# A pre-activation convolution on one core: transformed planes and sums with the columns outside and the row quadruples inside, and signs written to PSUM in f32

## The reference

```
v  = group_norm(x)                        # 32 groups of 8 channels, each image by itself
xn = batch_norm(v) * gamma + beta         # over all 16 images
t  = where(xn > 0, 1, -1)                 # signs
y  = conv3x3(t, w) + b                    # 256 -> 256 channels, padding 1
s  = sum over channels of |clip(xn, -1, 1)|
beta_map = (conv3x3(s, ones) + bb) / (conv3x3(256, ones) + bb)
out = x + y * beta_map
```

## Time and profile before

| | |
|---|---|
| median of 3 runs | 922.34 us (922.2 to 922.56) |
| the profiled execution: its own time | 922.45 us |
| its span, first to last instruction | 920.7 us |
| TensorE matmul busy | 789.4 us, 86% |
| VectorE busy | 769.4 us, 84% |
| ScalarE busy | 621.5 us, 68% |
| GpSimd busy | 140.6 us, 15% |

### The profile page before, as it was taken

The page is one execution under the profiler, slowest core; times in us unless marked ns, Lnnn a source line. Parts: engine busy times, 40 slices in busy tenths (PEclk is TensorE's granted clock), DMA queues, the critical chain, the costliest instruction groups (busy, mean ns, idle before and its releaser), DMA issues.

```text
span 920.7 us, 12815 instructions
## 1 busy us (share of the span) xinstructions
PE 789.4 (86%) x4722; PEld 468.2 (51%) x4722; DVE 769.4 (84%) x1193; ACT 621.5 (68%) x514; POOL 140.6 (15%) x158
## 2 busy tenths in 40 slices
PE   2100019999999999999999999999999999999996
PEld 1100015555555555555555555555555555555553
DVE  4899689999797979888888888797978787879756
ACT  2365738978685868677777777777778685858411
POOL 0089400011010111111111100111111111101011
PEclk9655559999999999999999999999999999999998
DMA  9999962489797979888788888796969696958578
GB/s 358 430 429 429 412 287 80 145 257 306 213 284 197 265 217 253 240 237 226 247 231 246 238 221 270 190 306 164 320 157 313 170 294 186 289 164 214 138 211 245
DMA packets 45446, 232.00 MB, mean 252 GB/s; under 512 B 11504, under 2 KB 12528, under 8 KB 41328
## 3 DMA queue, kind: packets, MB, share of 16 engines
q0 software_dynamic: 17856, 99.56, 41.9%
q1 hardware_dynamic: 26800, 132.05, 39.3%
q10 hardware_dynamic: 768, 0.12, 0.1%
HBM read 179.92 MB, written 51.79 MB: 252 GB/s over the span
## 4 chain that ended last, share of the span: by engine, by line
PE 79%; DVE 8%; DMA 5%; POOL 5%; ACT 2%; issue 1%; SPq 0%; DVEq 0%; ACTq 0%; POOLq 0%
PE acc L633 78%; DMA y<-x 3%; DVE st L762 2%; DMA xb<-x 2%; POOL V L328 1%; POOL U L345 1%; DVE st L775 1%; ACT U L414 1%; DVE y L1001 1%; DVE y L990 0%; POOL V L333 0%; POOL V L340 0%; POOL V L335 0%; DVE D L909 0%; POOL V L338 0%
## 5 line engine op out<-in xcount | busy, mean ns | idle before, releaser
L633 PE MATMUL acc<-V,U 128*128 128x385 f16 (+1 forms) x4608 | 768.2, 330 | 1.0 <-DVE y L990 0.6
L633 PEld LDWEIGHTS acc<-V,U 128*128 128x128 f16 x4608 | 450.5, 98 | 314.3 <-issue 1.9
L486 ACT ACTIVATE sn<-acc,inv_s 128x784 f32<-128x784 f32 x126 | 115.1, 914 | 193.2 <-PE acc L633 187.1
L355 POOL DMA_DIRECT2D y<-x x62 | 53.5, 862 | 710.5 <-DVE y L1001 697.0
L1001 DVE SCALAR_TENSOR_TENSOR y<-y,vec,bmap 128x1568 f32<-128x1568 f32 x63 | 115.6, 1834 | 0.1
L464 ACT ACTIVATE r<-xb,ab 128x1568 f32<-128x1568 f32 x64 | 106.6, 1690 | 5.5 <-ACT u L439 4.0
L439 ACT ACTIVATE u<-xb,ab 128x1624 f16<-128x1624 f32 x63 | 109.1, 1732 | 0.1
L449 ACT ACTIVATE T<-u 128x1680 f16<-128x1680 f16 x60 | 95.6, 1594 | 1.7 <-DVE D L909 1.7
L452 ACT ACTIVATE T<-T 128x1568 f16<-128x1568 f16 x58 | 87.6, 1510 | 1.8
L909 DVE TENSOR_TENSOR D<-T 128x1568 f16<-128x1568 f16 x62 | 60.4, 974 | 15.5 <-ACT T L452 15.3
L603 PE MATMUL csum<-mv,cst 128*128 128x32 f32 x2 | 0.6, 396 | 84.6 <-DVE mv L750 84.6
(11 more groups left out here) (127 smaller groups left out, 457.4 us busy)
## 6 DMA issues: line engine op xcount, KB each, us to landing
xb<-x SPq DMA_DIRECT2D x60, 812.0 KB, 6.3
y<-x POOLq DMA_DIRECT2D x62, 784.0 KB, 8.1
out<-y POOLq DMA_DIRECT2D x62, 784.0 KB, 9.8
y<-x SPq DMA_DIRECT2D x16, 1568.0 KB, 9.7
bmap<-map_rows SPq DMA_DIRECT2D x32, 784.0 KB, 6.0
xb<-x SPq DMA_DIRECT2D x14, 1568.0 KB, 10.8
V<-w_t SPq DMA_DIRECT2D x2, 1152.0 KB, 14.8
xb<-x SPq DMA_DIRECT2D x4, 420.0 KB, 9.2
```

What stands on the lines that cost most here:

```text
L486: nc.scalar.activation(sn[:, b, half], acc[:, b, :, 0:N], ACT.Copy, scale=inv_s[:, b:b + 1])\
L633: return nc.tensor.matmul(by_row(acc[:, g % 2, bank, 0:N])[:, :, lo:hi], U[:, ci, digits, k, dx, co * P:(co + 1) * P], by_row(V[:, a, ci, ...
```

## The change

The transformed data of images 1 to 15 get another order of their columns. Where a plane was 7 rows (q) of 56 columns (w), it now has 56 columns outside and the 7 quadruples inside (`w q` in place of `q w`). One column is then 7 neighbouring elements, and a matmul with `dx = 0` or `dx = 2` reads and writes one run of 385. Image 0 keeps the old order.

- ScalarE writes the signs of images 1 to 15 to PSUM, in f32, to one buffer `su` (31 rows, 1736 elements), in place of two f16 buffers in SBUF. So `sign` waits until the planes of the group before were made.
- `planes` reads `su` with `row_taps`: 6 taps x 56 columns x 7 quadruples, 2352 elements with a step of 4 rows inside, where it read 1680 elements in order. It writes them as `taps` to `T` without gaps.
- VectorE's `transform` has the same instructions with the same counts of elements, on whole blocks of 392.
- Snapshots (`snapshot`, and the last ones at L579) read `acc` with a step of 7 elements and write `sn` in row order. `ends` reads `acc` with that step.
- `csum` and `box` now share a bank with the end of `su`. So `quarter_sums(m)` has a new wait on TensorE: for the planes of group 3 of image m (L449), or in image 0 for the first sign of image 1.
- In the hand-written start ScalarE's order changes: `sign(1, 1, 1)` moves behind `planes(1, 0)`, `snapshot(0, 2, 0)` moves ahead of `absolute(1, 1, 1)`, and `planes(1, 3)` moves ahead of `channel_sums(1)`. In image 1 TensorE runs `quarter_sums` behind `third` (`late_sums`), and its loop starts one image later.
- The edge rows of `su` are set once at the start, and the warm-up matmuls write to `unused`.

```diff
+        low = ctx.enter_context(nc.psum_tensor("low", [P, 4 * 512], F32))
+        su = low[:, 0:UR * W].rearrange("p (r w) -> p r w", w=W)
+        unused = low[:, W:W + N]
+        csum = low[:, UR * W + W:UR * W + W + NI * CT]
...
+        def row_taps(g):
+
+            base = su[:, g // 2:g // 2 + HR + 2]
+            return bass.AP(base.tensor, base.offset, [list(base.ap[0]), [W, K6], [1, W], [4 * W, Q]])
...
-                at_least(act, t_ready, s - 1)
-                nc.scalar.activation(u[:, g % 2, 1:1 + XR], by_row(xb[:, c, g // 2]),
+                if isinstance(m, int) and m == 0:
+                    signs = u[:, c]
+                else:
+                    signs = su
+                    if not (isinstance(m, int) and s == G4):
+                        act.wait_ge(t_ready, s)
+                nc.scalar.activation(signs[:, 1:1 + XR], by_row(xb[:, c, g // 2]),
...
-                nc.scalar.activation(T[:, 30:60], u[:, g % 2, h:h + HR + 2], ACT.Relu, scale=2.0).then_inc(t_ready, 1)
+                nc.scalar.activation(taps[:, 2:8].rearrange("p k (w q) -> p k w q", q=Q), row_taps(g), ACT.Relu,
+                                     scale=2.0).then_inc(t_ready, 1)
...
+                sums, kept = acc[:, b, :, 0:N], sn[:, b, half]
+                if not (isinstance(n, int) and n == 0):
+                    sums = sums.rearrange("p k (w q) -> p k q w", q=Q)
+                    kept = kept.rearrange("p k (q w) -> p k q w", w=W)
+                nc.scalar.activation(kept, sums, ACT.Copy, scale=inv_s[:, b:b + 1]).then_inc((snap1, snap2)[half], 1)
...
-            sign(1, 1, 1)
             snapshot(0, 1, 1)
             planes(1, 0)
+            sign(1, 1, 1)
             absolute(1, 1, 0)
+            snapshot(0, 2, 0)
             absolute(1, 1, 1)
-            snapshot(0, 2, 0)
             channel_sums(0)
...
             def quarter_sums(m):
 
+                if isinstance(m, int) and m == 0:
+                    pe.wait_ge(u_ready, G4 + 1)
+                else:
+                    pe.wait_ge(t_ready, 4 * m + 4)
...
+                if isinstance(n, int) and n == 0:
+                    into = by_row(acc[:, g % 2, bank, 0:N])[:, :, lo:hi]
+                    plane = by_row(V[:, a, ci, VPLANE[k], h])[:, :, lo + dx - 1:hi + dx - 1]
+                else:
+                    into = acc[:, g % 2, bank, Q * lo:Q * hi]
+                    plane = V[:, a, ci, VPLANE[k], h, Q * (lo + dx - 1):Q * (hi + dx - 1)]
...
-                    if g == 0:
+                    if g == 0 and not late_sums:
                         quarter_sums(n)
                     third(n - 1, 1 - a, 3) if g == 0 else third(n, a, g - 1)
+                    if g == 0 and late_sums:
+                        quarter_sums(n)
...
+                nc.vector.tensor_tensor(diff[:, 0], taps[:, 4:8], taps8, ALU.subtract).then_inc(cq_done, 1)
...
+                nc.vector.tensor_tensor(V[:, a, c, 2:5:2, h], diff[:, :, 2], diff[:, :, 1], ALU.add)
+                nc.vector.tensor_tensor(V[:, a, c, 3:6:2, h], diff[:, :, 2], diff[:, :, 1], ALU.subtract)
+                nc.vector.tensor_tensor(V[:, a, c, 0:2, h], diff[:, 0, 2:4], diff[:, 0, 0:2], ALU.subtract)\
                   .then_inc(v_ready, 1)
...
-                        out=quads(y[:, g])[:, :, 3 * k], in0=by_row(acc[:, b, k, 0:N]), scalar=scale[:, b:b + 1],
+                        out=quads(y[:, g])[:, :, 3 * k], in0=row_order(n, acc[:, b, k, 0:N]), scalar=scale[:, b:b + 1],
```

More of the change, by code:

```diff
@@ L535, in begin @@
                 snapshot(n, 0, 0)
-                channel_sums(n)
                 if late_planes:
                     planes(n, 3)
+                channel_sums(n)
                 sign(n + 1, 1 - a, 0)
@@ L613, in keep_busy @@
                 for _ in range(count):
-                    nc.tensor.matmul(box[:, 0:N], U[:, 0, 0, 0, 0, 0:P],
+                    nc.tensor.matmul(unused, U[:, 0, 0, 0, 0, 0:P],
                                      U[:, 0, 0, 0].rearrange("p b o -> p (b o)")[:, 0:N], start=True, stop=True)
@@ L683, in third, with image @@
                 products(n, a, g, THIRD, third_done)
-            def image(n, a, final=False):
+            def image(n, a, final=False, late_sums=False):
                 for g in range(G4):
@@ L718, in _ @@
             second(0, 0, 3)
-            with pe.Fori(0, (NI - 2) // 2) as i:
-                image(2 * i + 1, 1)
+            image(1, 1, late_sums=True)
+            with pe.Fori(0, (NI - 4) // 2) as i:
                 image(2 * i + 2, 0)
+                image(2 * i + 3, 1)
+            image(NI - 2, 0)
             image(NI - 1, 1, final=True)
@@ L890, in first_group, with first_differences @@
                 nc.vector.tensor_tensor(plane(0), d[:, 0, 2:HR:4], d[:, 0, 1:HR:4], ALU.add).then_inc(v_first, 1)
-            def differences(m, g, d):
-                h, s = g // 2, 4 * m + g
+            def first_differences(g, d):
+                h = g // 2
                 pair = lambda at: T[:, at:at + 62].rearrange("p (j r) w -> p j r w", j=2)[:, :, 0:28:4]
[L896 to L900, removed]
+                at_least(dve, cq_done, g)
+                dve.wait_ge(u_ready, g)
+                nc.vector.tensor_scalar(T[:, 30:60], u[:, g % 2, h:h + HR + 2], 0.0, 2.0, ALU.max, ALU.mult)\
+                  .then_inc(t_ready, 1)
+                dve.wait_ge(t_ready, g + 1)
+                nc.vector.tensor_scalar(T[:, 1:28:2], T[:, 31:58:2], 2.0, None, ALU.mult).then_inc(t4_ready, 1)
+                nc.vector.tensor_scalar(T8[:, :], T[:, 30:30 + HR], 4.0, 3.0, ALU.mult, ALU.subtract)\
+                  .then_inc(t8_ready, 1)
+                dve.wait_ge(t4_ready, g + 1)
+                nc.vector.tensor_tensor(rows(d[:, 1], 1), pair(3), pair(1), ALU.subtract).then_inc(aq_done, 1)
+                dve.wait_ge(t8_ready, g + 1)
+                nc.vector.tensor_tensor(d[:, 0], T[:, 32:32 + HR], T8[:, :], ALU.subtract).then_inc(cq_done, 1)
@@ new lines, in first_other_planes, with first_transform @@
+            def first_other_planes(g, d):
+                nc.vector.tensor_tensor(v_planes(0, g, 3, 2), d[:, :, 2:HR:4], d[:, :, 1:HR:4], ALU.subtract)
+                nc.vector.tensor_tensor(v_planes(0, g, 0, 1), rows(d[:, 0], 2), rows(d[:, 0], 0), ALU.subtract)\
+                  .then_inc(v_ready, 1)
+            def first_transform(g):
+                at_least(dve, v_ready, g)
+                first_differences(g, D)
+                dve.wait_ge(cq_done, g + 1)
+                dve.wait_ge(aq_done, g + 1)
+                nc.vector.tensor_tensor(v_planes(0, g, 2, 2), D[:, :, 2:HR:4], D[:, :, 1:HR:4], ALU.add)
+                first_other_planes(g, D)
@@ L911, in first_planes @@
[L911 to L920, removed]
-                  .then_inc(v_ready, 1)
@@ L923, in transform @@
-            def transform(m, a, g):
-                at_least(dve, v_ready, 4 * m + g)
-                differences(m, g, D)
-                if not (isinstance(m, int) and m <= 1):
-                    dve.wait_ge(third_done, 4 * m - 6 + 2 * (g // 2))
-                first_planes(m, a, g, D)
-                other_planes(m, a, g, D)
+                nc.vector.tensor_tensor(diff[:, 0], taps[:, 4:8], taps8, ALU.subtract).then_inc(cq_done, 1)
+                if not (isinstance(m, int) and m <= 1):
+                    dve.wait_ge(third_done, 4 * m - 6 + 2 * h)
```

51 lines of the change are left out of this document (30 added, 21 removed).

## The result

The changed kernel takes 917.92 us (median of 5 runs, 917.55 to 918.94), the kernel before 922.20 us in the runs beside it. The ratio is 0.9954, with a 95% interval from 0.9942 to 0.9965: 4.3 us or 0.46% faster. Forecast were 916.6 us and a gain of 5.7 us.

The account below looks back on a forecast made before the run. TensorE's own pace was taken to bound the main loop, VectorE the stretch before 214 us. From 922.34 us, -7.0 for edge matmuls, 0 for ScalarE, +1.3 for the start and 0 for the end gave 916.6; range 913.5 to 926.5.

Parts of the forecast that it names:

- Term 1: TensorE's edge matmuls behind 214 us: one run paying 386 columns saves 2.5 ns on each of 2800, -7.0 us.
- 2.8 ns left over: TensorE's matmuls: time beyond the columns' own, 166.1 ns each against 392 / 2.4 = 163.3 ns.
- 166 and 167 ns: Centre and edge matmul times read from two short trace windows, taken to speak for equal cost.
- Term 2: ScalarE in the loop: longer planes, 2.18 us against 1.594, +0.58 a group, all hidden; sum 0.
- the cover ahead of `quarter_sums`: TensorE's new wait for planes of group 3: about 0.5 us left, the thinnest cover of all.
- the price of ScalarE's step: ScalarE's strided reads: priced at nothing, from VectorE's L957 taking the expected 345 ns with a step.
- Term 3: The start, where VectorE has no slack: waits for the sums' rows cost +1.3 us together (0 to 4).
- (a): Start, channel_sums(0): sums come later, at about 174.8 us, so VectorE waits 0 to 1.8 us, say 0.8.
- (b): Start, channel_sums(1): now at about 199.4 us, behind planes(1, 3) and late quarter_sums; 0 to 2 us, say 0.5.
- B: Rival on the edge matmuls: one run of 385 costs what seven of 55 did; 923.6 us, chance 0.16.
- C: Rival on ScalarE: strided PSUM reads take a second cycle per element; 935 to 963 us, or 964; chance 0.14.
- D: Rival on the start: longer waits and a further one in pair_sum, 6 us or more; 922 to 927, chance 0.05.

Follow-up runs that it names:

- runs55_again: Changed kernel with edge matmuls of images 1 to 15 back to 7 runs of 55 at a distance of 56; 923.81 us, ratio 1.0018 to the kernel before.
- signs_sbuf: Changed kernel with the signs in f16 in the two SBUF buffers of the kernel before, read with the same step of 4 rows; 985.23 us.
- run384: Changed kernel with the single run of an edge matmul cut from 385 to 384 columns, with an even start in the bank; 917.95 us.
- finish_late: Changed kernel with VectorE's beta_map of image 1 and finish(0, 2) both moved behind ends(1, 0); 919.80 us, ratio 0.9971 to the kernel before.

## Why the prediction held

**Term 1, the edge matmuls: right in size, 0.2 ns too large, and for a reason that didn't hold.** A piece was to take 47.36 us and took 47.40. That is 2.3 ns an edge matmul in place of 2.5, or -6.4 us for 2800 of them in place of -7.0. A run of 55 does pay for 56, and one run of 385 for 386. But it is not the count that is rounded: runs of 54 would then have saved 5.8 ns, and saved 0.4. Columns are paid in aligned pairs on both sides, and since the tap shifts one side against the other, an even run pays a pair more as well. That both reasons give 56 for a run of 55 is luck. The "2.8 ns left over" was 2.5, and 0.8 more behind two of each six matmuls. The "166 and 167 ns" read from the earlier trace rows should be 165 and 167.5, from 0.33 / 2 and 0.67 / 4; the trace's own starts, to 1 ns, give 166.5 and 166.0 for these two windows, which is within the rounding that the prediction named.

The Trainium skill's N / 2.4 GHz + 2.5 ns (TensorE: Matmul & The Clock Gate, "Wait — 56ns, not 53.3ns?") fits the measured 165.8 ns of 392 columns in one run, and the 160.0 ns of 378 columns with both sides even. For 385 its plain N gives 162.9 and the trace 164.0; counted in pairs it would be 163.3, and the other 0.6 stay open.

**Term 2, ScalarE: right, with some luck.** L471 was put at 2.18 us and takes 2.12; the cover ahead of `quarter_sums` was put at 0.5 us and is 0.58, and TensorE doesn't wait there. Snapshots, `ends` and the transform kept their times, and `runs55_again` shows the loop's piece unchanged, to 0.01 us, with all of ScalarE's and VectorE's edits in. The luck is in the price of ScalarE's step, nothing. The one row it rested on, L957, is VectorE's, and it reads `crow`, which the DMA leaves in SBUF. In `signs_sbuf` ScalarE pays double for a step in SBUF, so that row says nothing of ScalarE; what made the price right is that the signs lie in PSUM, and no row of before had tested this.

**Term 3, the start: right in its sum by luck, wrong in its parts, and one part missing.** (a) was to cost 0.8 us and cost nothing: the sums came at 174.57 and the rows were in by 178.01. (b) was to cost 0.5 and cost 1.29, since the load of the rows, issued at 200.14, took up to 7.5 us; that the transfers of x and y beside it made it so long was assumed and not tested. The two errors cancel: the start moved by 1.43 us in place of 1.3. What was left out is TensorE's clock, which fell to 1.2 GHz for 3.4 us behind the wait of 2.05 us, another 1.7 us in the profiled execution. The wait of before, of 0.56 us ahead of 213.99, had no such sequel. This is most of the difference between the forecast 5.7 us and the profiled 3.6. That the scatter of the five runs, 1.4 us, is the same clock falling in some of them and not in others isn't shown, though it fits: the mean granted clock is 0.936 in the two longest (918.88 and 918.94 us) and 0.938 to 0.941 in the three others. It can't be all of it: without its 1.7 us the profiled execution would have taken 917.2, and the shortest took 917.55.

**The rivals.** B (one run pays as seven) is out by the piece. C (a second cycle for strided reads of PSUM) is out by L471 and L512. Its price would have been near for SBUF: (4287 - 2122) / 2352 = 0.92 ns more per element. D was the right place, with VectorE's wait there; the start cost 1.4 us, and 3.1 with the clock that D didn't name, where D put 6 or more.

The Trainium skill's rule for SBUF, that two hits to a line are needed for full rate (Advanced Engine Details and Errata, "SBUF Cachelines"), agrees with the 4287 ns of ScalarE. It doesn't show on VectorE, whose L1012 takes 346 ns (L957 345) with 58 elements of f32 from one that it reads to the next. Its rule for PSUM (same page, "PSUM Cachelines"), on which C rested, does not show on ScalarE or VectorE here.

## What to carry to other kernels

Count TensorE's columns in aligned pairs, run by run and on both sides, before a layout is chosen: with a shift by one column seven even runs of 54 paid seven pairs more (5.8 ns), and one long run pays one. A run of odd length, as the 55 here, pays for the even count either way. A reordering with long steps was free for ScalarE where it read f32 from PSUM, and doubled its time where it read f16 from SBUF. Where a hand-written start hangs on one busy engine, put its waits for DMAs behind the work that others wait for, and measure each further move: the two tried here brought the wait back later, and longer.

## What was not expected of the hardware

- Seven runs of 54 columns cost 165.8 ns a matmul when the two sides start one column apart, and 160.0 when both start even.
- The step of 4 rows: 2352 elements in 4287 ns from SBUF in f16, in 2122 ns from PSUM in f32.
- TensorE's clock fell to 1.2 GHz for 3.4 us behind a wait of 2.05 us in the changed kernel, with 16 us of matmuls without a gap ahead of it, behind 2.06 us in `run384` and behind 1.99 us in `finish_late`. In `runs55_again` a wait of 2.00 us at the same place had no such sequel, as its 28.07 us show. So the length of the wait doesn't decide it alone.
